# A transformer block on one core: the attention loop in another order on all four engines

## The reference

```python
q, k, v = (cproj(Wq), cproj(Wk), cproj(Wv))          # of the layer-normed x
qr = q * phase[None]; kr = k * phase[None]           # rotation by the position
E = jnp.exp(jnp.clip(-mu[:, None, None] * dt[None], MIN_EXP, 0.0))
s = jnp.einsum('bihd,bjhd->bhij', qr, jnp.conj(kr)).real
qn = (q.real ** 2 + q.imag ** 2).sum(-1); kn = (k.real ** 2 + k.imag ** 2).sum(-1)
V = (sigma_sq / (2.0 * mu))[:, None, None] * (1.0 - E * E) + (eta_sq + gamma_sq)[:, None, None]
maha = jnp.maximum(qn[..., None] + (E * E)[None] * kn[:, :, None, :] - 2.0 * E[None] * s, 0.0) / V[None]
logits = coef * jnp.log1p(maha / nu[None, :, None, None]) - 0.5 * DH_ * jnp.log(V)[None]
A = jax.nn.softmax(jnp.where(causal, logits, -jnp.inf), axis=-1)
out = jnp.einsum('bhij,bjhd->bihd', A, v)            # then y @ Wo
x = x + layernorm(attention(layernorm(x)))
x = x + layernorm(ffn(layernorm(x)))                 # h = silu(gate) * up, then down
```

## Time and profile before

| | |
|---|---|
| time, median of 3 runs | 1975.73 us (1973.03 to 1975.79) |
| the profiled execution, its own time | 1975.62 us |
| its span | 1973.8 us |
| mean granted clock of TensorE | 0.978 of full speed |
| busy over the span: PE, DVE, ACT, POOL | 92%, 81%, 80%, 74% |

### The profile page before, as it was taken

How to read it: one execution, slowest core, us unless ns; L and a number is a source line. 1 busy time by engine, 2 the same in 40 slices (tenths; PEclk the granted TensorE clock), 3 DMA queues, 4 the chain that set the end, 5 groups by cost and what they waited for, 6 DMA issues and landing times. The chain is left out here.

```text
span 1973.8 us, 41342 instructions
## 1 busy us (share of the span) xinstructions
PE 1815.5 (92%) x10660; PEld 1491.2 (76%) x10660; DVE 1601.2 (81%) x3834; ACT 1577.3 (80%) x3217; POOL 1460.0 (74%) x1257
## 2 busy tenths in 40 slices
PE   0379999999999999999999999999999999997997
PEld 0348878887878788878788788878887888876886
DVE  6358878887878788878878888878888888895884
ACT  2748878888878888888888888888887888886554
POOL 1368878887878788887878788878887888872654
PEclk9979999999999999999999999999999999998998
DMA  8823111311131113111131113111310111110111
GB/s 178 288 81 108 37 44 44 108 43 59 44 104 36 50 44 101 50 59 44 53 100 39 42 44 108 43 59 44 108 43 25 42 43 43 43 45 21 44 44 43
DMA packets 65071, 128.18 MB, mean 65 GB/s; under 512 B 14449, under 2 KB 44657, under 8 KB 55921
## 3 DMA queue, kind: packets, MB, share of 16 engines
q1 hardware_dynamic: 64880, 126.01, 20.7%
HBM read 107.24 MB, written 25.03 MB: 67 GB/s over the span
## 5 line engine op out<-in xcount | busy, mean ns | idle before, releaser
L567 POOL TENSOR_TENSOR qk<-rm 64x512 f32<-64x512 f32 x512 | 693.7, 1355 | 110.9 <-PE ps L764 50.0
L577 POOL TENSOR_TENSOR ek<-tabs,kn 128x512 f32<-128x512 f32 (+3 forms) x512 | 462.8, 910 | 145.1 <-DVE lg L1426 100.3
L724 PE MATMUL pa<-xt,wt 128*128 128x512 f32 x1536 | 443.4, 425 | 13.9 <-DVE rm L1401 7.0
L1434 DVE CUSTOM_DVE_ANT_0 lg<-lg,tabs,ncog 128x512 f32<-128x512 f32 (+3 forms) x512 | 437.0, 872 | 0.0
L1426 DVE CUSTOM_DVE_ANT_0 lg<-ps,ek,qb 128x512 f32<-128x512 f32 (+3 forms) x512 | 279.5, 546 | 150.9 <-POOL ek L577 106.8
L1401 DVE TENSOR_TENSOR rm<-pa,tabs 128x512 f32<-128x512 f32 x512 | 332.5, 677 | 75.0 <-POOL qk L567 69.9
L764 PE MATMUL ps<-qk 128*128 128x512 f32 (+3 forms) x1024 | 375.7, 451 | 8.9 <-DVE lg L1426 6.2
L788 PE MATMUL py<-pt,vt 128*128 128x128 f32 x2560 | 350.5, 276 | 0.1
L788 PEld LDWEIGHTS py<-pt,vt 128*128 128x128 f32 x2560 | 333.8, 193 | 17.0 <-issue 0.3
L724 PEld LDWEIGHTS pa<-xt,wt 128*128 128x128 f32 x1536 | 287.5, 195 | 71.9 <-issue 14.1
L1082 ACT ACTIVATE lg<-lg,qb 128x512 f32<-128x512 f32 (+3 forms) x512 | 278.8, 558 | 35.5 <-DVE lg L1426 31.6
(11 more groups left out here) (156 smaller groups left out, 2155.8 us busy)
## 6 DMA issues: line engine op xcount, KB each, us to landing
xt<-xs_d SPq DMA_DIRECT2D x62, 1024.0 KB, 4.8
tabs<-vec_d SPq DMA_DIRECT2D x64, 192.0 KB, 4.7
xs_d<-xt SPq DMA_DIRECT2D x8, 1024.0 KB, 5.6
wt<-wraw_d SPq DMA_DIRECT2D x8, 768.0 KB, 7.7
acc<-in_L_attn_x SPq DMA_DIRECT2D x8, 512.0 KB, 7.4
tabs<-rope_d SPq DMA_DIRECT2D x16, 256.0 KB, 5.8
tabs<-in_L_attn_x SPq DMA_DIRECT2D x8, 512.0 KB, 4.7
out<-tabs SPq DMA_DIRECT2D x8, 512.0 KB, 3.1
```

The costliest lines, as they stand in the source:

```text
L567: pool.tensor_tensor(qk[part * DH:(part + 1) * DH, z * HH + hh, :], rm[row, 2 * part, :], rm[row, 2 * part + 1, :], ALU.add if part else A ...
L577: pool.tensor_tensor(ek[:, n % 2, 0:w], tab(par, hh, E2_T, N - w), kn[:, hh, 0:w], ALU.mult).then_inc(ek_pool, 1)
L724: last = mm(pa[r][:, :], wproj(par, z, kt, a, r * P, (r + 1) * P), xt[slot][:, kt, b, :], start=(n == 0), stop=(n == 3 * KT - 1))
L1434: dve.tensor_tensor_reduce(lg[:, hh, at(n)], lg[:, hh, at(n)], tab(par, hh, T3_T, N - w), ncog[:, par, 0, hh:hh + 1], 3e38, ALU.add, ALU.m ...
```

## The change

Every engine's `body`, the few calls ahead of the loop and the run-out behind it are written in another order. No helper is changed, and none is called more or less often. The bodies are also cut at another place: before, an iteration's first score tiles, three distances and two logarithms are done in the body of the iteration ahead of it; after, only the first two score products, one decay and one decayed norm are. The core of the difference, with a line on the place ahead of each piece:

```diff
@@ ACT, body @@
+                log(c, 0, 0, it.slot)
+                log(c, 0, 1, it.slot)
+                log(c, 0, 2, it.slot)
+                if nxt:
+                    square(cn, 1, 0)
+                if old:
                     keep_turned(cp, 1, 1)
-                    exp(cp, 1, 3)
-                if nxt:
-                    square(cn, 1, 0)
-                if old:
                     keep_turned(cp, 1, 2)
...
-                exp(c, 1, 0)
-                keep_values(c, it.slot, 1)
-                log(c, 1, 3, it.slot)
-                keep_turned(c, 0, 0)
@@ DVE, end of the body @@
                     add_output(cp, it.b_before, 1, 0)
+                logits(c, 0, 1, it.par)
+                logits(c, 0, 2, it.par)
+                logits(c, 0, 3, it.par)
                 if nxt:
                     decay(cn, 0, 0, it.behind)
+                if old:
+                    add_output(cp, it.b_before, 1, 1)
+                if nxt:
                     bounds(cn, it.behind, 1 - it.slot)
-                    distance(cn, 0, 0, 1 - it.slot)
-                    decay(cn, 0, 1, it.behind)
-                logits(c, 1, 2, it.par)
-                if nxt:
-                    distance(cn, 0, 1, 1 - it.slot)
-                    decay(cn, 0, 2, it.behind)
-                if old:
-                    add_output(cp, it.b_before, 1, 1)
-                if nxt:
-                    distance(cn, 0, 2, 1 - it.slot)
@@ PE, end of the body @@
                     f_transposes(0)
+                if old:
+                    out_project(cp, it.before, 1, 0)
                 if nxt:
                     norms_k(cn)
-                if old:
-                    out_project(cp, it.before, 1, 0)
-                if nxt:
                     scores(cn, 0, 0)
+                if old:
+                    out_project(cp, it.before, 1, 1)
+                if nxt:
+                    scores(cn, 0, 1)
                     norm_q(cn)
-                    scores(cn, 0, 1)
-                if old:
-                    out_project(cp, it.before, 1, 1)
-                turn(c, 0, 1)
-                if nxt:
-                    scores(cn, 0, 2)
@@ POOL, body @@
-                pool.wait_ge(rot_pool[1], c[4] + 4)
                 if it.raw is not None:
                     low_weights(pool, 1 - it.par, it.ready)
                 if it.opens is not None:
                     pool.wait_ge(grp[it.behind], it.opens)
+                decay_norm(c, 0, 1, it.par)
+                decay_norm(c, 0, 2, it.par)
+                pool.wait_ge(ek_pool, c[8] + 3)
+                rotated(c, 1, 1, 1)
                 decay_norm(c, 0, 3, it.par)
                 decay_norm(c, 1, 0, it.par)
@@ PE, run-out @@
+            out_project(c, 1, 0, 0)
+            attend(c, 1, 0, 1)
             turn(c, 1, 2)
             gate_up(0, 0)
-            attend(c, 1, 0, 1)
             turn(c, 1, 3)
             gate_up(0, 1)
-            out_project(c, 1, 0, 0)
@@ DVE, run-out @@
             split_low(0)
+            residual(1)
+            logits(c, 1, 2, 1)
+            logits(c, 1, 3, 1)
             add_output(c, B - 1, 0, 0)
             inverse(c, 1)
-            residual(1)
```

More of the change, by code:

```diff
@@ L609, in body @@
                     pool.wait_ge(ek_pool, c[8] + 6)
-                    rotated(cn, 0, 0, 1)
+                    rotated(cn, 0, 0, 0)
                 decay_norm(c, 1, 2, it.par)
@@ L626, in body @@
                 if nxt:
+                    pool.wait_ge(ek_pool, c[8] + 8)
+                    rotated(cn, 1, 0, 0)
+                    sum_squares(cn, 1)
+                    pool.wait_ge(sum_pool, cn[2] + 2)
+                    rotated(cn, 1, 0, 1)
+                    rotated(cn, 1, 1, 0)
                     decay_norm(cn, 0, 0, it.behind)
-                    decay_norm(cn, 0, 1, it.behind)
-                    decay_norm(cn, 0, 2, it.behind)
-                    pool.wait_ge(ek_pool, cn[8] + 3)
-                    rotated(cn, 1, 1, 1, True)
             pool.wait_ge(grp[0], 16 * TABLE_LOADS)
@@ L865, in body @@
                     pe.wait_ge(w_lo, it.ready)
+                if old:
+                    turn(cp, 0, 0)
+                    turn(cp, 0, 1)
                 if nxt:
@@ L898, in body @@
                 if old:
+                    turn(cp, 1, 3)
                     attend(cp, 1, 1, 1 - it.slot)
                     attend(cp, 1, 2, 1 - it.slot)
+                    out_project(cp, it.before, 0, 1)
+                    attend(cp, 1, 3, 1 - it.slot)
                 values(c, it.par, it.slot, 0)
                 values(c, it.par, it.slot, 1)
-                if old:
-                    attend(cp, 1, 3, 1 - it.slot)
-                    out_project(cp, it.before, 0, 1)
-                turn(c, 0, 0)
                 if not nxt:
                     f_transposes(0)
-                if nxt:
-                    norms_k(cn)
                 if old:
@@ L1533, in body @@
                     start(it.fresh, it.behind)
-                decay(c, 0, 3, it.par)
-                distance(c, 0, 3, it.slot)
+                if old:
+                    logits(cp, 1, 0, it.before)
+                distance(c, 0, 0, it.slot)
+                if old:
+                    logits(cp, 1, 1, it.before)
+                    inverse(cp, 0)
+                    logits(cp, 1, 2, it.before)
+                decay(c, 0, 1, it.par)
+                decay(c, 0, 2, it.par)
+                distance(c, 0, 1, it.slot)
+                if nxt:
+                    rotate(cn, it.behind, 0, RC)
+                distance(c, 0, 2, it.slot)
                 if old:
@@ L1540, in body @@
                     first_norm(0)
+                decay(c, 0, 3, it.par)
                 if nxt:
-                    rotate(cn, it.behind, 0, RC)
                     rotate(cn, it.behind, 0, IS)
-                if old:
-                    inverse(cp, 0)
+                distance(c, 0, 3, it.slot)
                 if nxt:
                     rotate(cn, it.behind, 0, RS)
-                    rotate(cn, it.behind, 0, IC)
                 decay(c, 1, 0, it.par)
-                logits(c, 0, 0, it.par)
-                logits(c, 0, 1, it.par)
+                if not nxt:
+                    residual(0)
                 distance(c, 1, 0, it.slot)
@@ L1554, in body @@
                 distance(c, 1, 1, it.slot)
-                logits(c, 0, 2, it.par)
-                logits(c, 0, 3, it.par)
+                if nxt:
+                    rotate(cn, it.behind, 0, IC)
+                decay(c, 1, 2, it.par)
+                logits(c, 0, 0, it.par)
+                if old:
+                    add_output(cp, it.b_before, 0, 0)
+                distance(c, 1, 2, it.slot)
                 if not nxt:
-                    residual(0)
-                decay(c, 1, 2, it.par)
+                    second_move(0)
+                if old:
+                    inverse(cp, 1)
                 if nxt:
                     rotate(cn, it.behind, 1, RC)
-                distance(c, 1, 2, it.slot)
-                if old:
-                    add_output(cp, it.b_before, 0, 0)
+                decay(c, 1, 3, it.par)
                 if nxt:
                     rotate(cn, it.behind, 1, IS)
-                logits(c, 1, 0, it.par)
-                if old:
-                    inverse(cp, 1)
-                if not nxt:
-                    second_move(0)
-                logits(c, 1, 1, it.par)
-                if nxt:
                     rotate(cn, it.behind, 1, RS)
                     rotate(cn, it.behind, 1, IC)
+                distance(c, 1, 3, it.slot)
                 if old:
@@ L1595, in body @@
                 if nxt:
-                    distance(cn, 0, 2, 1 - it.slot)
+                    bounds(cn, it.behind, 1 - it.slot)
             def start(g, par):
@@ L1641, in _ @@
             add_output(c, B - 1, 1, 1)
-            second_move(1)
             dve.wait_ge(acc_dve, 4 * B * G + 4)
```

120 lines of the change are left out of this document (52 added, 68 removed).

## The result

The changed kernel takes 1999.29 us in the median of 4 runs (1994.9 to 2000.54), beside 1974.38 us for the kernel before on the same chip (4 runs, 1971.31 to 1975.79). The ratio is 1.0124 (95% interval 1.0104 to 1.0145): slower by 25 us, where 60 were forecast. The profiled execution is the quickest of the four, 1994.9 us, with a span of 1993.1 us, 19.3 more than before. That kernel's median lies between 1972.9 and 1975.9 us by the chip, so a difference between two experiments is good to some 3 us.

A forecast was written before the change was run, and what follows sets the result against it. PE was taken as the bound, at 25.0 us of work per 25.11 us iteration. Tail +73, weights iterations -10 and run-out -6, taken as +60 on 1975.7, gave 2035 us, with a range of 1955 to 2065.

The forecast's parts named there:

- Still less likely to be the next bound: ACT, busy 80% before, loses two of four table loads (164 us); none of it counted, since PE does not wait.
- The mechanism: At the tail, POOL operations block three DVE logits, delaying the bounds; PE's first projection starts 1.5 us late each iteration.
- N+1.9: End of POOL's last rotation, 1.9 us after the next iteration's key norms start (N); possible range N+1.4 to N+2.2.
- 52 x 1.4: Tail stall over 52 regular intervals, each 26.5 us, 1.4 more than now: +73 us.
- both delays are there in every iteration: Reason for the late rotation end: POOL's chain is held by a late decayed norm (c,1,0) and by logits (c,0,0).
- Rival B: Tail with one block instead of three, rotation ending before N+1.59, PE 0.2 us late: 1964 us; chance 0.20.
- Weights iterations: Seven iterations that split weights fall from 30.6 to about 29.3 us, POOL's split standing where there is slack: -10 us.
- Run-out: Behind the loop: last key norms to third gate product falls from 55.2 to about 50 us: -6, give or take 5.
- Ahead of the loop: nothing: The start, ahead of the loop: no change in time counted.
- D: Same three blocks, plus a lower PE clock after the gap in every iteration, 52 x 1.5 more: 2113 us; chance 0.05.
- C: Tail free of blocks, PE at its own 25.0 us per iteration: 1950 us; chance 0.14.
- E: Something off the path decides all; removed table loads never held PE, time the same, 1970 to 1980 us; chance 0.05.

The follow-up runs named there:

- e8: Kernel before with the logarithms computed as plain sums (Identity) on ACT, so no table loads in the loop: 1972.85 us, ratio 1.0000.
- e11: Changed kernel with POOL's decayed norm (cn,0,0) ahead of the body's last rotation, plus a one-column exponential on ACT forcing two more table loads per iteration: 2016.67 us, ratio 1.0211.
- e3: Changed kernel with PE's query norms moved right behind score (cn,0,0), ahead of output projection (cp,1,1) and score (cn,0,1): 1995.43 us, ratio 1.0100.
- e1: Changed kernel with DVE's logits (c,0,2) and (c,0,3) moved behind the bounds instead of ahead of the decay: 1978.69 us, ratio 1.0021.
- e2: Changed kernel with POOL's decayed norm (cn,0,0) ahead of the body's last rotation instead of behind it: 1952.0 us, ratio 0.9884 to the kernel before.
- e9: Changed kernel with DVE's logits (c,0,0) moved behind the addition (cp,0,0) and the distance (c,1,2): 2019.05 us, ratio 1.0235.
- e7: Changed kernel with POOL's split of the next weights moved back to just ahead of the decayed norm (c,0,3): 1995.97 us, ratio 1.0149.
- e6: Kernel before with only the run-out reordered on PE and DVE, the last iteration's first output projection ahead of the first gate product: 1970.09 us, ratio 0.9980.
- e5: Changed kernel with POOL's decayed norm (cn,0,0) ahead of the last rotation, and DVE's distance (c,0,0) ahead of logits (cp,1,0): 1974.43 us, ratio 1.0005.
- e4: Changed kernel with a one-column exponential on ACT between logarithms (c,0,2) and (c,0,3), forcing two more table loads per iteration: 2083.53 us, ratio 1.0542.

## Why the prediction came out as it did

**PE as the bound, and the loads that go.** Right for the kernel before: e8 takes all four loads out of it and nothing moves. "Still less likely to be the next bound" was too easy, though: in the changed order ACT's chain between the logarithms and the turned copies is tight, and two more loads in it cost 1.0 us per iteration (e11). The saved loads were not worth time by themselves, but the new order has no room for them at that place; another place was not tried.

**The tail.** The mechanism held. The stall is at the first projection and put down to the bounds; the three logits take 1.40, 1.48 and 1.07 us where 1.2, 1.4 and 1.1 were named; e3 excludes the query norms, e1 removes the stall from DVE's side, and e2 removes it by POOL's order alone. The Trainium skill, SBUF — State Buffer, section Who interferes with whom, has a DVE instruction with two SBUF inputs and a GpSimd instruction that reads SBUF exclude each other, the second to issue blocking entirely; the trace agrees, in the stall's three rows and in e2. The last rotation's end, taken as N+1.9, is N+1.87 in these tails. The rule that a later rotation costs more holds as well, within this kind: ending at N+2.10 to 2.19 (e9) it gives a stall of 1.5 us, not the 1.8 worked out for N+2.2.

**The size.** The term that was off most is "52 x 1.4": the 51 regular intervals and the two of 27.9 gave +47 instead of +73. Two steps of it failed. First, within a tail with three blocks the stall is 1.2 us and not 1.5: each of the six steps on DVE was rounded up a little (together 0.3), and PE's nominal start is N+5.08 and not 4.97. Over 52 intervals that is some 16 of the 26 us. Second, "both delays are there in every iteration" was wrong, and it makes the other 10. One tail was worked out and multiplied, while there are four kinds. The rule of the last paragraph also turns round once logits 1 issues between two rotations: at N+2.64 the stall is 0.8. Rival B's condition held for the five tails that end by N+1.41; they cost less than it priced (25.0 us for its 25.2). What makes the kinds alternate is not settled. Logits (c,0,0), the one cause that was tried, changes how often each kind comes, and is not the whole of it (e9).

Three smaller slips stand beside these. Behind the first interval there are 53 regular ones, 7 with weights and 2 at jumps, not 52, 7 and 3. The earliest end of the last rotation, from N-13.9 and 15.4 us of chain, is N+1.5 and not N+1.4. And for the weights iteration a shift of -1.4 against +1.4 of the tail leaves 30.6; how the text comes to 29.3 can't be followed.

**Weights iterations.** -10 forecast, -15 measured, and by another way. The step, that POOL's split now stands where there is slack, is refuted by e7, and e8 excludes the loads in the old order. What the prediction left out of this term is the clock, which in the change stays at 1.00 through all seven. Laid matmul by matmul, start to start, beside a regular iteration, the one of before at 871.73 is 5.5 us late: 3.9 from waits, and 1.6 because PE works at the lower clock behind the gap. The one of after at 882.18 is 3.5 late, all of it waits. So of the 2.1 us between them 1.6 is the clock and only about 0.4 the waits. Over the seven, interval times what is missing to full clock is 15.4 us before and 0 after, an upper estimate, beside the 15.0 gained. The longest wait of PE in the iteration before is 2.36 us, and after it is

```profile
894.88 0.49 PE L756 MATMUL ps<-qk 128*128 128x128 f32 x2 [1.73 <-DVE lg L1416]
```

Whether it is this shorter wait that keeps the clock up is not shown.

**Run-out and start.** -6 forecast, -5.0 measured; that the step named brought it is not shown (e6), so the near hit may be luck. DVE's wait of 9 us, said to go, became two of 2.07 and 5.89. "Ahead of the loop: nothing" missed the first interval, 5.4 us shorter: in it PE works at a mean clock of 0.79 before and 0.92 after, by the same estimate 4.2 us of the 5.4. The jumps, counted at nothing, gave 3.3, with clocks of 0.89 and 0.94 before and 1.00 and 0.94 after. These gains and the weights make 29 us, where 16 were forecast. So the forecast misses by 26 us in the tail and by 13 in the other terms, mostly where the clock came back, for which the sum had none.

**The rivals.** D was given 5% as a rule for every iteration, and that did not come; but it happens now and then. Both intervals of 27.9 us have it. PE at such a stall, and the windows behind:

```profile
729.96 1.63 PE L716 MATMUL pa<-xt,wt 128*128 128x512 f32 x4 [1.04 <-DVE qb L1399]
```

```profile
730.00:732.00 2.00, 2.00 (x6) 1.62 (x7) 1.66 (x4) 1.84 (x4) 0.15 (x1) 0.63 0.00 0
732.00:734.00 2.00, 2.00 (x9) 1.62 (x8) 1.89 (x7) 1.60 (x5) 1.84 (x2) 0.51 0.00 0
```

These two intervals are 1.4 and 1.6 us longer than others of the kind at full clock (for the first, those that also come second behind a weights iteration). In the slower runs of the change, 4 to 6 us above the profiled one, the mean granted clock is 0.983 to 0.988 instead of 0.989, so there may be more of them; no profile of those shows it. C and E did not come.

## What to carry to other kernels

Where a DVE instruction and a POOL instruction exclude each other, an instruction's price is set by the other engine's order: look at the order in which the two issue around the place that the bound engine waits for, and move the one that has slack (one swap in e2 took 47 us off the change). Finishing something earlier can cost time, if it releases an operation that then blocks (e5). A stall worked out for one iteration is not to be multiplied until several neighbouring ones have been worked out with the state that each leaves to the next. And when two orders are compared, compare the granted clock too, stretch by stretch: here the change lost 47 us in the tail and won, by estimate, about half of it back in stretches where the clock no longer fell.

## What was not expected of the hardware

- A stall on PE of the same length is not always followed by the same clock. Of the 31 tails of the change with three blocks (recorded waits of 0.95 to 1.3 us) 29 are followed by the full clock and 2 by 0.51 to 0.64 in the two 2 us windows behind. In e3 it is 0 of 30, in e7 4 of 37 and in e9 8 of 43. The price is 1.4 to 1.6 us each time.
- In the seven weights iterations the clock falls every time before (longest wait 2.36 us in the one shown) and never in the change (1.73).
- A logits issued between two rotations of POOL takes 0.61 us, and the two rotations then 2.98 instead of 2.61: the POOL operation is held up in its turn, by 0.4 us.
- The same logits, 128 wide, takes 0.35 us free and up to 1.42 blocked in the change; over the kernel the 512 logits range from 309.6 us (e1) and 358.9 (e2) to 509.8 (e4), with the same data and shapes.
